# F32R products that nobody reads in TensorE's waits between the scan and the experts, and the residual rows' products in halves by channel

## What is computed

```python
x = x + tanh(g_xattn) * ssm(ctx_1024, layernorm(x))        # scan over 256 positions, 16 states, 256 channels
h = layernorm(x)
logits = h @ gate_w                                        # (1024, 8)
top_logits, top_idx = top_k(logits, 2)
top_w = softmax(top_logits)
for e in range(8):
    out += cw[:, e] * ((silu(h @ w0[e]) * (h @ w1[e])) @ wo[e])
x = x + tanh(g_ffn) * out
```

## Time and profile before

| what | value |
|---|---|
| median of three runs | 299.03 us |
| profiled execution, its own time | 299.81 us |
| its span, first to last instruction | 298.0 us |
| busy: TensorE, VectorE, ScalarE, GpSimd | 89%, 78%, 62%, 59% of the span |
| mean granted TensorE clock | 0.956 of 2.4 GHz |
| chain that ended last: TensorE's share | 62% |

### The profile page before, as it was taken

The page is one execution under the profiler, slowest core; times in us unless marked ns, Lnnn a source line. Parts: engine busy times, 40 slices in busy tenths (PEclk is TensorE's granted clock), DMA queues, the critical chain, the costliest instruction groups (busy, mean ns, idle before and its releaser), DMA issues.

```text
span 298.0 us, 4632 instructions
## 1 busy us (share of the span) xinstructions
PE 264.1 (89%) x1158; PEld 178.3 (60%) x1159; DVE 231.5 (78%) x406; ACT 185.1 (62%) x343; POOL 175.4 (59%) x159
## 2 busy tenths in 40 slices
PE   7985696999889898978989899999999999999970
PEld 7432342343335352523576667989898989898850
DVE  2989999999999999999859539888665656565630
ACT  2895759766685658778488215565657575756540
POOL 6103288999999998999500321546564656465242
PEclk9999799999999999999978669999999999999996
DMA  7699300000000001000198401242333333343322
GB/s 237 211 390 387 143 2 0 1 0 0 0 1 2 1 0 70 0 0 3 45 347 278 142 21 34 38 69 41 67 45 63 51 57 53 53 55 51 36 25 31
DMA packets 16678, 22.74 MB, mean 76 GB/s; under 512 B 2570, under 2 KB 10290, under 8 KB 16658
## 3 DMA queue, kind: packets, MB, share of 16 engines
q1 hardware_dynamic: 11472, 16.41, 15.7%
q0 software_dynamic: 4416, 6.03, 12.9%
q10 hardware_dynamic: 770, 0.06, 0.2%
HBM read 17.38 MB, written 5.11 MB: 75 GB/s over the span
## 4 chain that ended last, share of the span: by engine, by line
PE 62%; DVE 15%; issue 11%; POOL 6%; ACT 3%; POOLq 1%; DVEq 0%; ACTq 0%
PE PD L1046 11%; PE PZ L1086 11%; PE PU L1046 10%; PE PY L860 7%; DVE states L1255 5%; POOL hC L421 5%; PE PY L1072 4%; DVE states L1261 3%; PE PZ L1037 2%; PE PZ L921 2%; PE PY L855 1%; PE PU L768 1%; PE PD L805 1%; PE PY L1029 1%; PE PU L846 1%
## 5 line engine op out<-in xcount | busy, mean ns | idle before, releaser
L421 POOL TENSOR_TENSOR hC<-states,WO 128x512 f32<-128x512 f32 x63 | 79.9, 1280 | 15.1 <-PE PY L860 10.1
L1261 DVE TENSOR_TENSOR_SCAN states<-PD,states 128x512 f32<-128x512 f32 x64 | 77.6, 1214 | 1.1 <-ACT PD L629 0.9
L860 PE MATMUL PY<-hC,ident 128*128 128x512 f32 x128 | 67.5, 610 | 4.1 <-POOL hC L421 4.0
L456 POOL DMA_INDIRECT out<-lg,y_at x23 | 37.2, 1618 | 49.1 <-ACT lg L734 41.2
L629 ACT ACTIVATE PD<-WO,Aneg 128x510 f32<-128x510 f32 x64 | 43.9, 689 | 18.6 <-DVE states L1261 15.5
L442 POOL DMA_INDIRECT hC<-x_rows,x_at x23 | 27.2, 1183 | 33.7 <-DMA x_rows<-u 19.5
L1255 DVE TENSOR_TENSOR states<-PU,WO 128x512 f32<-128x512 f32 x64 | 42.9, 672 | 1.2 <-POOL hC L421 1.0
L718 ACT ACTIVATE hidT_hi<-PY 128x512 fp32r<-128x512 f32 x23 | 13.8, 600 | 38.7 <-PE PY L1072 38.7
L1510 DVE TENSOR_TENSOR WO_lo<-WO,WO_hi 128x512 fp32r<-128x512 f32 x46 | 29.7, 688 | 6.1 <-issue 5.7
L860 PEld LDWEIGHTS PY<-hC,ident 128*128 128x128 f32 x128 | 22.5, 191 | 16.6 <-POOL hC L421 11.2
L1498 DVE TENSOR_TENSOR dA<-PU,dA 128x512 f32<-128x512 f32 x23 | 15.9, 691 | 21.1 <-PE PU L1046 21.1
(11 more groups left out here) (238 smaller groups left out, 513.1 us busy)
## 6 DMA issues: line engine op xcount, KB each, us to landing
W<-in_L_ffn_w SPq DMA_DIRECT2D x16, 512.0 KB, 10.5
WO<-in_L_ffn_wo SPq DMA_DIRECT2D x8, 512.0 KB, 6.2
xs<-in_x SPq DMA_DIRECT2D x2, 512.0 KB, 5.5
out<-xs SPq DMA_DIRECT2D x2, 512.0 KB, 3.1
early<-in_ctx SPq DMA_DIRECT2D x1, 512.0 KB, 4.3
x_rows<-u SPq DMA_DIRECT2D x1, 512.0 KB, 6.0
x_rows<-u SPq DMA_DIRECT2D x2, 256.0 KB, 2.7
hC<-x_rows,x_at POOLq DMA_INDIRECT x23
```

The costliest lines, as they stand in the source:

```text
L421: pool.tensor_tensor(hC[:, n % 2, :], states[:, n % RING, :], C_rep[:, pair % C_RING, :], ALU.mult).then_inc(hc_done, 1)
L456: pool.indirect_dma_start(out=out, out_offset=bass.IndirectOffsetOnAxis(ap=y_at[:, s:s + 1], axis=0), in_=y_tile[s % 2], in_offset=None, c ...
L860: pe.matmul(PY[:, h, :], ident[:, :], hC[:, n % 2, :], start=False, stop=(m == DS - 1)).then_inc(y_done, 1)
L1261: dve.tensor_tensor_scan(states[:, n % RING, :], DEC[n % 2], states[:, n % RING, :], 0.0, ALU.mult, ALU.add).then_inc(scan_done, 1)
```

## The change

`spin` goes, and `fill` comes in: products of 512 columns in F32R (one instruction each) of the upper part of a weight with itself, whose result nobody reads. It stands in seven places, with counts of its own: `gated` ahead of the second pair's router, `mask` ahead of `ranks`, `places` behind them, `rows` between the four groups of the table's products, `weights` behind the table, `table` between the groups of the weights' products, and `turn` behind `x_turn(0)`. Until the table is made, the fills write into TABLE's bank (PU[1]), later into PD[1]. The residual rows' products of the second pair are made by `gated_rows(r, h)`, two for each half of the channels, and the first of them stand between the two halves of the router.

```diff
-SPINS = (4, 1, 2)
+FILL = {"gated": 3, "mask": 3, "places": 17, "rows": 1, "weights": 6, "table": 1, "turn": 3}
...
-            def spin(times):
-
-                for _ in range(times):
-                    pe.matmul(PD[1][:, :], ident[:, :], W1_hi[:, 0, 0, :].bitcast(F32), start=True, stop=True)
+            def fill(place, to):
+
+                for _ in range(FILL[place]):
+                    pe.matmul(to, W1_hi[:, 0, 0, 0:P], W1_hi[:, 0, 0, :], start=True, stop=True)
+
+            def gated_rows(r, h):
+
+                pe.wait_ge(gz_ok, 2 + h + 1)
+                x2 = PZ[r][:, :].rearrange("p (l e h) -> p l h e", l=2, h=2)
+                for l in range(2):
+                    mm = pe.matmul(x2[:, l, h, :], z_cols[:, QBLK + 2 * r + h, l, :], scaled_id[:, :],
+                                   start=(r == 0), stop=(r == 0 or (h == 1 and l == 1)))
+                if h:
+                    mm.then_inc(x2_ps, 1)
 
             pe.wait_ge(scan_done, NT)
             pe.wait_ge(W_hi_ok, 1)
-            router(1, 0)
-            router(1, 1)
-            pe.wait_ge(base_kept, 2)
-            for r in range(QB):
-                add_gz(1, r)
             pe.wait_ge(dbu_done, NT)
             pe.wait_ge(c_ok, NT // 2)
+            fill("gated", TABLE)
+            router(1, 0)
+            pe.wait_ge(base_kept, 2)
+            gated_rows(0, 0)
+            router(1, 1)
+            gated_rows(1, 0)
+            gated_rows(0, 1)
+            gated_rows(1, 1)
+            fill("mask", TABLE)
             ranks()
-            pe.wait_ge(neg_ok, 2)
-            pe.wait_ge(gz_ok, 2 * NQ)
-            pe.wait_ge(logits_ok, 2 * NQ)
-            spin(SPINS[0])
-
-            pe.wait_ge(slot_id_ok, 1)
+            fill("places", TABLE)
+
+            pe.wait_ge(slot_id_ok, 1)
             pe.wait_ge(logits_ok, 2 * NQ)
             n = NQ * TOPK * QBLK
             for j in range(n):
                 if j % 4 == 0:
+                    if j:
+                        fill("rows", PD[1][:, :])
                     pe.wait_ge(row_hot_ok, j // 4 + 1)
...
             mm.then_inc(table_ps, 1)
-            spin(SPINS[1])
+            fill("weights", PD[1][:, :])
             pe.wait_ge(slot_w_ok, 2)
             for j in range(n):
+                if j and j % 4 == 0:
+                    fill("table", PD[1][:, :])
...
-            spin(SPINS[2] // 2)
             x_turn(0, 0, 16)
-            spin(SPINS[2] - SPINS[2] // 2)
+            fill("turn", PD[1][:, :])
             pe.wait_ge(slots_ok, 1)
```

More of the change, by code:

```diff
@@ L919, in add_gz @@
                     for h in range(2):
-                        alone = q == 1 and r == 0
-                        mm = pe.matmul(x2[:, l, h, :], z_cols[:, q * QBLK + 2 * r + h, l, :], scaled_id[:, :],
-                                       start=alone, stop=(alone or (l == 1 and h == 1)))
+                        mm = pe.matmul(x2[:, l, h, :], z_cols[:, q * QBLK + 2 * r + h, l, :], scaled_id[:, :], start=False, stop=(l == 1 and h == 1))
                 mm.then_inc(x2_ps, 1)
```

## The result

The changed kernel takes 297.03 us, the median of 20 runs (295.35 to 301.88), against 298.87 for 20 runs of the kernel before (296.91 to 300.16). The ratio is 0.9935 with a 95% interval of 0.9918 to 0.9953: 1.8 to 1.9 us faster, about half of the 3.6 that 295.4 asked for, and inside the stated range. A ratio leaves out executions more than 1.5% above the fastest of their kernel, here the one at 301.88 us. The profiled execution took 295.49 us, with a span of 293.7.

The account below looks back on a forecast made before the run. Bound by VectorE's routing chain up to the table, then by TensorE alone. Weights 1.1, spins 1.7 and 0.8, `gate(0)` 0.9, `x_turn(0)` 0.2, front 0.2, less 0.4: 299.81 - 4.5 = 295.3, stated as 295.4 us, range 293.8 to 298.4.

Parts of the forecast that it names:

- The logits stay where they were: Router: 0.48 us of residual products added, about 0.5 saved by full clock, so logits stay at 153.39 us.
- the 0.48 us for four instructions: Two residual products ahead of the router's second half add four instructions at 0.119 us each to the path.
- The table ends 0.2 us late against its rows: Table: single fills make a group 0.67 us against a `row_hot` piece every 0.60 to 0.63, ending about 0.2 later.
- 4.5 forecast: End of `gate(0)`: 171.8 us with the second `x_turn`, 4.5 earlier than before, and carried through to the kernel's end.
- the 0.78 us: Profiled execution of before lay 0.78 us above the runs' median; the forecast did not take this off again.
- `x_turn(0)` near 168.9: Behind the weights' products: `x_turn(0)` starts near 168.9 us, 3.0 earlier, with its gathered rows landed by 168.7.
- VectorE's 0.38 us: Ahead of `over`: VectorE's 0.38 us wait for the count goes, bringing stored rows and gather 0.38 earlier.
- rival (c): Clock holds, but stores beside an earlier load, or the gather, take up to 2 us more: 297.1 us, chance 0.09.
- the clock holds: The forecast case: full clock from 149 to 155 us and through the weights' products, giving 295.4 us; chance 0.52.
- rival (d): Front fills do not hold the clock at 152; table starts 0.5 to 0.9 us late: 296 to 298, chance 0.10.
- Rival (b): Clock falls behind the 17 fills or inside the table, stays half until behind `gate(0)`: 301.1 us, chance 0.09.
- The gap of 2.0 us behind the 17 fills: Ahead of the table: fills end near 159.9, table begins at 161.9, leaving TensorE idle 2.0 us; named as the danger.

Follow-up runs that it names:

- the whole rows: Changed kernel with both halves of the router ahead of all residual products: 296.82 us; the same with 25 fills behind the ranks: 295.30 us.
- the later load: Changed kernel with SP's load of the third pair of wo blocks held until ScalarE's copy of the last residual rows is done: 297.04 us.
- the spins elsewhere: Kernel before with its F32 spins put six behind the ranks, two behind the table, none around `x_turn(0)`: 296.73 us.
- 25 fills: Changed kernel with 25 instead of 17 fills behind the ranks, run twice: 295.33 and 295.03 us.
- without the inner fills: Changed kernel with 25 fills behind the ranks and none inside the table or the weights' products: 296.18 us.

## Why the prediction was right, and where it was off

**Right.** The mechanism and its prices. A fill costs 0.23 us at full clock (17 from 157.99 to 161.9; 25 in 5.77 us), as forecast from the experts' products; the 131 ns of the Trainium skill ("TensorE: Matmul & The Clock Gate", "Back-to-back issue gap") are refuted for this shape and type by the same rows. The logits stay where they were (8.26 us behind the last scan for 8.31); the whole rows' kernels confirm the 0.48 us for four instructions ahead of the router's second half (0.43 and 0.44). The table ends 0.2 us late against its rows (wait of 0.22 ahead of `x_at`). Table and weights cost 0.112 a product (a group of four and a fill begins every 0.68 us). In the traces the start of the experts moved by 4.0 us, of 4.5 forecast. That the profiled execution then came within 0.2 us of the sum (295.49 for 295.3) is partly luck: from the last scan to the end of the span it is 4.8 us shorter than before, 0.8 of it behind the start of the experts, where the forecast had nothing, and the scan itself ended 0.5 later.

**The step that was off most: from the trace to the median.** The sum was made for the profiled execution (299.81 - 4.5 = 295.3) and its result, 295.4, given as the median. So the 0.78 us by which that execution lay above the median was already out of the gain that was forecast against the median (3.6 us and not 4.5). What went wrong is the reason given for stopping there: that with the clock held the spread between executions would be gone. It is not. The 18 runs of the changed kernel at 0.976 to 0.979 lie between 295.35 and 298.14 us, and their kernel's median is 1.54 us above the execution that the sum describes. The clock does make a part of the spread of before: of 81 runs of that kernel beside the experiments, the 48 with a mean clock of 0.962 or less have a median of 299.1 us, the 33 with more 298.3. No trace of a usual run of the changed kernel was taken, so where it loses the 1.5 us stays open.

**In the sum: `x_turn(0)` near 168.9.** That is 23.8 us behind the last scan; measured 24.67. The term was the stored rows, which were to shift with VectorE's 0.38 us. They were ready to be stored 0.2 earlier, but the store took 3.44 us and not 2.57 (from the issue at 18.2 to the landing at 20.7 us behind the last scan). That is rival (c) in a small form, but the load issued earlier, named there, does not explain it (see the later load). The traces point to the instruction fetch beside the store, which no step of the prediction had. In the four kernels where the fetch does not meet the store, `x_turn(0)` is at 23.3 to 23.8. (It is at 23.8 with the spins elsewhere too, where the fetch does meet it.)

**And "the clock holds", given 0.52 as one case.** It held through the weights, but not throughout: in the changed kernel's trace 3.4 us of the stage are at half, in the three with 25 fills and the inner ones none. They fall at 153.8 under the residual rows, in spite of the `gated` fills (rival (d)), which put the ranks at 157.4 and not 155.4, and so VectorE's wait ahead of `over` shrank to 0.21 us and did not go. In the trace with the later load they fall over `gate(0)`, which no rival had in that form. Rival (b), given 0.09 and 301.1 us, is what the trace of the whole rows shows, if at 298.97 us; runs with a mean clock as low are one of 20 here (301.88 us), two of 12 with the later load and three of 12 with the whole rows. The gap of 2.0 us behind the 17 fills, named as the danger, is 1.26 and 1.50 us in two traces, and closing it brings 1.7 to 2.0 us; by which way it does is the open question.

**Open.** How much of the 1.7 to 2.0 us of the 25 fills is the clock and how much the store. Single traces give sizes, by the second `x_turn` behind the last scan: 26.5 us with 25 fills; 27.3 in the changed kernel, with the slow store and the clock full behind it; 27.5 without the inner fills, with the quick store and the clock at half over `gate(0)`; 27.9 with the later load, with both. So, in single traces, the store costs some 0.8 us and the clock 1.0, and how often each occurs in the runs without a trace is not known. A kernel that moves the fetch and leaves the clock alone was not run. Also open is why the fetch moved: the four kernels have in common eight instructions more on TensorE behind the ranks.

## What to carry to other kernels

Filler work for the clock should cover a wait to its end: here 17 products ended 1.3 to 1.5 us early in two traces, in both the clock fell later in the stage (1.4 and 7.1 us behind the gap), and fillers at half clock cost double, on the path; 25 products, of which the last end with the wait, were 1.7 to 2.0 us faster, at a price of 0.15 us. Judge it by the times and the mean granted clock of many executions, not by one trace, and measure from a fixed event rather than from the span's start. Don't take the gain of one trace for that of the median: here they were 4.3 and 1.8 us. Before adding fillers inside a chain of small products, try the ones that stand there already with other counts.

## What the runs showed of the hardware

- A fetch of 16 KB of instructions takes one of the 16 DMA engines for 0.9 to 1.7 us. In the ten traces where it falls beside two stores of 256 KB, these take 2.7 to 3.3 us as the median of the two, in the four where it comes before them 2.0 or 2.1. That the fetch is the cause is likely and not shown.
- The clock is lost at another place of the same stage from trace to trace: at 153.8 us in the changed kernel, at 161.9 with the whole rows, at 168.2 with the later load. Not all of the spread between executions is that: the 18 runs of the changed kernel at 0.976 to 0.979 still lie between 295.35 and 298.14 us, and only the one at 0.956 goes up to 301.88.
- With F32 products of 512 columns in the same waits (SPINS 6, 2, 0) the clock stays full from 157.0 to 170.6 us, as it does with F32R ones from 157.2 on. In the kernel without inner fills it fell at 170.0 us, behind 2.3 us of weights' products that keep TensorE busy for 1.97 of them; with the inner fills (2.48 of 2.50 us busy) it did not in three traces with 25 fills, but in the one with the later load it did (2.66 of 2.70 us busy just before).
